# Head sums of squares of four feature tiles on 32 columns each of TensorE, and a product that orders the rows

## What is computed

```python
q = silu(short_conv(x @ Wq + bq, q_conv)).reshape(B, S, h, d)
q = q / (norm(q, axis=-1) + 1e-06)
k = silu(short_conv(x @ Wk + bk, k_conv)).reshape(B, S, h, d)
k = k / (norm(k, axis=-1) + 1e-06)
v = silu(short_conv(x @ Wv + bv, v_conv)).reshape(B, S, h, d)
alpha = sigmoid(x @ Wa + ba)
beta = sigmoid(x @ Wb + bb)
out_gate = silu(x @ Wg + bg)
```

## Time and profile before

| | us |
|---|---|
| median of 3 runs (lowest to highest) | 3533.43 (3529.58 to 3539.18) |
| the profiled execution's own time | 3535.1 |
| its span | 3533.3 |
| TensorE busy in the span | 3299.1 (93%) |
| VectorE busy | 2739.6 (78%) |
| ScalarE busy | 1582.4 (45%) |
| GpSimd busy | 1845.0 (52%) |

### The profile page before, as it was taken

How to read it: one execution, slowest core, us unless ns; L and a number is a source line. 1 busy time by engine, 2 the same in 40 slices (tenths; PEclk the granted TensorE clock), 3 DMA queues, 4 the chain that set the end, 5 groups by cost and what they waited for, 6 DMA issues and landing times. The chain is left out here.

```text
span 3533.3 us, 191423 instructions
## 1 busy us (share of the span) xinstructions
PE 3299.1 (93%) x83236; PEld 2757.8 (78%) x83236; DVE 2739.6 (78%) x4491; ACT 1582.4 (45%) x2344; POOL 1845.0 (52%) x1707
## 2 busy tenths in 40 slices
PE   7999998799999999995999999999996997999999
PEld 5888886576766767674999999999995775888887
DVE  6767665787888878784899999999997866676765
ACT  4555553577777777773112121111213433545454
POOL 1232322465555665654787887888785431323232
PEclk8999999899999999997999999999997998999999
DMA  3122222232322323225677777777774772212121
GB/s 119 71 95 83 88 90 91 78 100 78 102 79 84 101 74 99 86 76 133 182 200 202 198 200 199 197 197 200 197 200 136 238 226 107 107 71 107 71 107 60
DMA packets 486526, 452.84 MB, mean 128 GB/s; under 512 B 55489, under 2 KB 448833, under 8 KB 467265
## 3 DMA queue, kind: packets, MB, share of 16 engines
q1 hardware_dynamic: 484160, 449.56, 42.1%
q10 hardware_dynamic: 2304, 2.49, 0.3%
HBM read 331.33 MB, written 120.60 MB: 128 GB/s over the span
## 5 line engine op out<-in xcount | busy, mean ns | idle before, releaser
L350 POOL TENSOR_TENSOR ffn_out<-ffn_gate,ffn_xres 128x512 f32<-128x512 f32 x128 | 223.5, 1777 | 779.8 <-DVE ffn_gate L254 779.4
L784 DVE SCALAR_TENSOR_TENSOR ain_conv<-ain_padded,ain_taps,ain_conv 128x512 f32<-128x512 f32 x384 | 416.8, 1085 | 13.8 <-DVE ain_tail L781 0.3
L1464 ACT ACTIVATE rec_u<-rec_ps_end 128x256 f32<-128x256 f32 x128 | 49.2, 384 | 645.7 <-PE rec_ps_end L1516 645.7
L885 POOL TENSOR_TENSOR ain_conv<-ain_conv,ain_term 128x512 f32<-128x512 f32 x192 | 272.4, 1419 | 16.0
L1232 POOL TENSOR_TENSOR rec_d_norm<-rec_dmat,rec_early 128x512 f32<-128x512 f32 x128 | 162.9, 1273 | 181.6 <-DVE rec_dmat L1314 181.6
L940 ACT ACTIVATE ain_buf<-ain_conv 128x512 f32<-128x512 f32 x192 | 121.0, 630 | 233.5 <-POOL ain_conv L885 147.6
L46 PE MATMUL ffn_ring<-ffn_mixkh,ffn_wkh 128*128 128x512 f32 x512 | 218.7, 427 | 6.5 <-DVE ffn_mixkl L196 6.5
L46 PE MATMUL ffn_ring<-ffn_mixrh,ffn_wrh 128*128 128x512 f32 x512 | 216.0, 422 | 9.2 <-DVE ffn_mixrl L306 9.2
L46 PE MATMUL ffn_ring<-ffn_mixkh,ffn_wkl 128*128 128x512 f32 x512 | 203.8, 398 | 0.0
L46 PE MATMUL ffn_ring<-ffn_mixrh,ffn_wrl 128*128 128x512 f32 x512 | 202.6, 396 | 0.0
L46 PE MATMUL ffn_ring<-ffn_mixkl,ffn_wkh 128*128 128x512 f32 x512 | 201.7, 394 | 0.0
(11 more groups left out here) (249 smaller groups left out, 10351.9 us busy)
## 6 DMA issues: line engine op xcount, KB each, us to landing
rec_early<-coeffs SPq DMA_DIRECT2D x512, 128.0 KB, 3.0
streams<-ain_buf SPq DMA_DIRECT2D x48, 1024.0 KB, 5.1
rec_qkv<-streams SPq DMA_DIRECT2D x126, 384.0 KB, 3.3
rec_qk_pe<-streams SPq DMA_DIRECT2D x127, 256.0 KB, 3.3
rec_late<-coeffs SPq DMA_DIRECT2D x504, 64.0 KB, 2.2
ffn_xres<-in_x SPq DMA_DIRECT2D x16, 1024.0 KB
ain_x<-x SPq DMA_DIRECT2D x16, 1024.0 KB, 4.9
gate<-ain_gate SPq DMA_DIRECT2D x16, 1024.0 KB, 6.7
```

The costliest lines, as they stand in the source:

```text
L350: added = nc.gpsimd.tensor_tensor(out[:, m, :], gate[:, m, :], xres[:, m, :], ALU.add)
L784: nc.vector.scalar_tensor_tensor(out=out[:], in0=pad[:, n:n + TOK], scalar=taps[:, u // KT, u % KT, n:n + 1], in1=out[:], op0=ALU.mult, op ...
L885: nc.gpsimd.tensor_tensor(out[:], out[:], term[:], ALU.add).then_inc(pool_conv, 1)
L1464: nc.scalar.activation(u[:], ps_end[:, :, 1, :], ACT.Copy).then_inc(u_ready, 1)
```

## The change

The head sums of a kind (q, then k) are now made together, after group u = 8 and after group u = 12. The matmul of feature tile m is 32 columns wide and writes rows 32m to 32m + 31 of `ps_rows`: sums of q on its first four rows, of k on its next four. The four of k accumulate onto those of q, in other rows. `sq` has five tiles in place of four, so that k's first square doesn't overwrite one of q; from k's second on a square waits for q's four sums. ScalarE's root now takes all 128 partitions, into a new tile `root`. After group u = 13 TensorE multiplies `root` by a matrix of zeros and ones, `in_rows`, which brings the 32 wanted rows to partitions 32 to 63 of `ps_rows` (`order_rows`), and VectorE's norms wait for that (`rows_ordered`) and read `ps_rows`. `gamma_norm` now lies in the place of `alpha`. The new constants are made with fewer memsets and four small copies out of `ident`.

```diff
@@ -557,13 +557,13 @@
         taps = sb("taps", [P, 3, KT, TAPS])
         mean_w = sb("mean_w", [P, P])
         start_mask = sb("start_mask", [P, NT, 3 * KT, TAPS - 1])
-        head_sum = sb("head_sum", [P, 2 * KT, P])
+        head_sum, in_rows = sb("head_sum", [P, 2, HD]), sb("in_rows", [P, P])
         not_first = sb("not_first", [P, TOK])
         x = sb("x", [P, KT, TOK])
         xc = sb("xc", [P, KT, TOK])
         xh = [sb(f"xh{s}", [P, KT, TOK], F32R) for s in range(2)]
         xl = [sb(f"xl{s}", [P, KT, TOK], F32R) for s in range(2)]
-        sq = sb("sq", [P, 4, TOK])
+        sq = sb("sq", [P, 5, TOK])
         half, half2 = sb("half", [P, 2, TOK]), sb("half2", [P, 2, TOK])
         sum1, sum2 = sb("sum1", [P, TOK]), sb("sum2", [P, TOK])
         ident, ones = sb("ident", [P, P]), sb("ones", [P, P])
@@ -710,10 +713,15 @@
                 nc.vector.tensor_tensor(W[n][1][:], stage[n], W[n][0][:].bitcast(F32), ALU.subtract).then_inc(w_split[n], 1)
 
             def select_heads():
-                for n in range(2 * KT):
+
+
+                for j in range(2):
                     for h in range(HG):
-                        col = (2 + n // KT) * H + h * KT + n % KT
-                        last = nc.vector.memset(head_sum[h * HD:(h + 1) * HD, n, col:col + 1], 1.0)
+                        nc.vector.memset(head_sum[h * HD:(h + 1) * HD, j, j * HG + h:j * HG + h + 1], 1.0)
+                cols = in_rows[:, 2 * H:4 * H].rearrange("p (j h g) -> p j h g", j=2, h=HG)
+                for m in range(KT):
+                    rows = slice(m * HD, (m + 1) * HD)
+                    last = nc.vector.tensor_copy(cols[rows, :, :, m], ident[rows, m * HD:m * HD + 2 * HG].rearrange("p (j h) -> p j h", j=2))
                 last.then_inc(heads_selected, 1)
 
             def place_ab():
@@ -798,8 +806,8 @@
                 nc.vector.tensor_copy(gamma_end[HROWS, :], gamma[HROWS, CH - 1:TOK:CH]).then_inc(ends_ready, 1)
 
             def norms(t):
-                dve.wait_ge(rooted, t + 1)
-                nc.vector.tensor_scalar_add(inv_norm[HROWS, :], inv_norm[HROWS, :], 1e-6).then_inc(padded_norm, 1)
+                dve.wait_ge(rows_ordered, t + 1)
+                nc.vector.tensor_scalar_add(inv_norm[HROWS, :], ps_rows[HROWS, :], 1e-6).then_inc(padded_norm, 1)
                 dve.wait_ge(padded_norm, t + 1)
                 nc.vector.reciprocal(inv_norm[HROWS, :], inv_norm[HROWS, :]).then_inc(norm_ready, 1)
                 dve.wait_ge(norm_ready, t + 1)
@@ -940,13 +948,13 @@
                 nc.scalar.activation(view, conv[u % 3][:].rearrange("p (c i) -> p c i", i=CH), ACT.Silu).then_inc(silued, 1)
                 if j < 2:
                     act.wait_ge(silued, 12 * t + u + 1)
-                    if u >= 4:
-                        act.wait_ge(heads_summed, 8 * t + u - 3)
-                    elif more:
+                    if u > 4:
+                        act.wait_ge(heads_summed, 8 * t + 4)
+                    elif u < 4 and more:
                         act.wait_ge(halved2, t + 2)
                     else:
                         act.wait_ge(heads_summed, 8 * t)
-                    nc.scalar.activation(sq[:, u % 4, :].rearrange("p (c i) -> p c i", i=CH), view,
+                    nc.scalar.activation(sq[:, u % 5, :].rearrange("p (c i) -> p c i", i=CH), view,
                                          ACT.Square).then_inc(q_squared, 1)
 
             def slot(t, s, more):
@@ -969,7 +977,8 @@
                     if more and u == 10:
                         high(t + 1, 1 - s)
                 act.wait_ge(heads_summed, 8 * t + 8)
-                nc.scalar.activation(inv_norm[HROWS, :], ps_rows[HROWS, :], ACT.Sqrt).then_inc(rooted, 1)
+                act.wait_ge(rows_ordered, t)
+                nc.scalar.activation(root[:], ps_rows[:], ACT.Sqrt).then_inc(rooted, 1)
                 silu(t, 10, more)
                 act.wait_ge(gate_stored, 16 * t)
                 act.wait_ge(w_split["g"], 1)
@@ -1016,12 +1025,18 @@
                 nc.tensor.matmul(ps_rstd[:], ones[:], rstd_diag[:].rearrange("p j n -> p (j n)"), start=True,
                                  stop=True).then_inc(spread_done, 1)
 
-            def head_sums(t, n):
-                pe.wait_ge(q_squared, 8 * t + n + 1)
-                if n == 0:
-                    pe.wait_ge(rooted, t)
-                nc.tensor.matmul(ps_rows[:], head_sum[:, n, :], sq[:, n % 4, :], start=(n == 0),
-                                 stop=(n == 7)).then_inc(heads_summed, 1)
+            def head_sums(t, j):
+
+                if j == 0:
+                    pe.wait_ge(padded_norm, t)
+                for m in range(KT):
+                    pe.wait_ge(q_squared, 8 * t + KT * j + m + 1)
+                    nc.tensor.matmul(ps_rows[m * HD:(m + 1) * HD, :], head_sum[:, j, :], sq[:, (KT * j + m) % 5, :],
+                                     start=(j == 0), stop=(j == 1), skip_group_check=True).then_inc(heads_summed, 1)
+
+            def order_rows(t):
+                pe.wait_ge(rooted, t + 1)
+                nc.tensor.matmul(ps_rows[:], in_rows[:], root[:], start=True, stop=True).then_inc(rows_ordered, 1)
 
             def slot(t, s, more):
                 pe.wait_ge(x_low, t + 1)
@@ -1041,8 +1056,10 @@
                     product(nc, ring[u % 4][:], *W["qkvg"[j]], m, xh[s], xl[s]).then_inc(group_done, 1)
                     if u == 5:
                         pe.wait_ge(heads_selected, 1)
-                    if 5 <= u < 13:
-                        head_sums(t, u - 5)
+                    if u in (8, 12):
+                        head_sums(t, u // 4 - 2)
+                    if u == 13:
+                        order_rows(t)
                     if more and u == 7:
                         var(t + 1)
                     if more and u == 11:
```

More of the change, by code:

```diff
@@ L578, in attn_in_phase @@
         alpha, beta, inv_norm = sb("alpha", [P, TOK]), sb("beta", [P, TOK]), sb("inv_norm", [P, TOK])
-        decay, gamma, gamma_norm = sb("decay", [P, TOK]), sb("gamma", [P, TOK]), sb("gamma_norm", [P, TOK])
+        decay, gamma, root = sb("decay", [P, TOK]), sb("gamma", [P, TOK]), sb("root", [P, TOK])
+        gamma_norm = alpha
         gamma_end = sb("gamma_end", [P, CPT])
@@ L605, in attn_in_phase @@
         q_squared, heads_summed, rooted = sem("q_squared"), sem("heads_summed"), sem("rooted")
+        rows_ordered = sem("rows_ordered")
         decay_ready, first_ready, scanned, padded_norm, norm_ready = (
@@ L695, in _ @@
             nc.vector.memset(head_sum[:], 0.0)
+            nc.vector.memset(in_rows[:], 0.0)
             nc.vector.memset(wab_pad, 0.0)
@@ L835, in _ @@
             weight_high("k")
+            dve.wait_ge(ident_step, 2)
             select_heads()
-            dve.wait_ge(ident_step, 2)
             deviations(0)
@@ L905, in square @@
                 act.wait_ge(centred, t + 1)
-                nc.scalar.activation(sq[:], xc[:], ACT.Square).then_inc(squared, 1)
+                nc.scalar.activation(sq[:, 0:KT, :], xc[:], ACT.Square).then_inc(squared, 1)
             def deviation(t):
```

## The result

| | us |
|---|---|
| changed kernel, median of 4 runs | 3637.96 (3633.78 to 3641.40) |
| kernel before, median of 4 runs beside it | 3536.30 (3529.58 to 3544.31) |
| ratio, 95% interval | 1.0293 (1.0280 to 1.0306) |
| the profiled execution's span | 3636.3 |

The change makes the kernel 2.9% slower, 101.7 us. The forecast was +68 (3601, range 3556 to 3632): the direction held, the size didn't, and the time lies above the range.

A forecast was written before the change was run, and what follows sets the result against it. Bound by the chain of ScalarE's shifts and silus and GpSimd's units, not TensorE. Fourteen intervals of 2.0 + 2.2 us (59), the last 7 and the end 2 gave +68 us: 3601 us, range 3556 to 3632.

The forecast's parts named there:

- What bounds the kernel: Slot of 61.33 us: a chain of ScalarE's shifts and silus and GpSimd's units 2, 5, 8 sets the pace, not TensorE.
- Head sums: TensorE's narrow sums: 1.2 us for four instead of 0.96 us each; the saving beside the chain, worth nothing by itself.
- The wait for the root: TensorE after group 13: idle 5.9 us (3.3), GpSimd's unit 2 3.8 us later, part given back, net +2.0 us a slot.
- The clock: TensorE's clock falls after the idle time, before the groups unit 2 needs: +2.2 us a slot, bounds 0 and +3.0.
- Normalising earlier: VectorE's lost wait for the spread of 1/std, 32.8 us in 14 waits: counted as nothing, VectorE waiting for ScalarE instead.
- The sum: Root to root: fourteen intervals of 4.2 us make 59, the last 7, the end 2; together +68 us.
- The rival of +99: Slots: no relief on GpSimd (+3.3) and 3.0 us from the clock, 3632 us; chance 0.05.
- The faster rival: TensorE's own work is the bound: 4.3 us less over 15 slots, 65 us, 3468 us; chance 0.06.
- The memsets: Before the first slot: fewer memsets save VectorE up to 3.9 us, covered by GpSimd's sums; otherwise under 3 us once.

## Why the prediction was wrong in its size

*What bounds the kernel.* Right. TensorE's 94% were no bound: 1 to 2 us less of its work a slot gained nothing, once with slots of 61.7 us and once with 59.1.

*Head sums.* The 1.2 us taken for four was 1.1 measured, where they didn't wait for a square. The packing section of the Trainium skill's page "TensorE: Matmul & The Clock Gate" has 2.38 times for three tiles of 32 columns; the 1.6 us for four worked out from it was an estimate, and the runs show less, 1.1. What the forecast had wrong here is the saving: 7.7 - 2.4 - 0.96 = 4.3 us by its working, 1.8 measured, since the wide sum costs 0.86 us between groups and not 0.96, and since the narrow ones seldom stand ready all four. It decides nothing.

*The wait for the root.* The idle time was forecast at 5.9 us and measured at 6.4. Group 14 was forecast to start 5.04 us late, and against the root it starts 5.16 late. The step that failed is the next one: "groups 14 and 15, `ps_ab` and the next slot's groups" are not all that is queued behind the wait. The mean product stands among them, between group 0 and group 1, and VectorE's centring waits for it. My sum had its 0.85 us, as the one float32 product, but not its reader. I had both facts in the description of the kernel and followed only the queue's groups, to shift(2). There the delay arrived as 3.8 us, and I let 1.8 of it be given back, 1.3 by GpSimd's units and 0.5 by silu(2). At the centring it arrives whole, at the head of the slot, so that ScalarE, VectorE and GpSimd shift together and meet each other as before: unit 2 took 9.3 us in the changed kernel, not 8.6, and nothing is given back.

*The clock.* Right as a mechanism, 1.5 us a slot in place of 2.2 (the mean product's 6.5 us less the 5.04 of queueing, and 68.3 less 66.8 with TensorE kept at work). Its size doesn't follow the length of the wait: 2 slow matmuls behind 6.4 us in the changed kernel, 5 to 7 behind 5.5 us with the mean ahead, 6 to 14 behind 4.0 us with the wait alone. What sets it stays open.

*Normalising earlier.* I had counted nothing for VectorE's lost wait for the spread. It cost: unit 9 of VectorE, from 1104.46 to 1109.90, moved into GpSimd's unit 8, which runs in the changed kernel from 1100.18 to 1109.35, 9.17 us,

```profile
1100.18 0.64 POOL L883 COPY ain_padded<-ain_tail 128x3 f32<-128x3 f32 x1 [4.26 <-ACT ain_conv L937]
...
1107.75 1.60 POOL L893 TENSOR_TENSOR ain_conv<-ain_conv,ain_term 128x512 f32<-128x512 f32 x1
```

and before from 1121.93 to 1130.57, 8.64 us, with VectorE's unit 9 only from 1128.64 on. That is +0.5 us a slot. It fits the version with the ordering product behind group 15, whose unit 8 takes 9.17 us too and whose slots are 61.7 and not 61.3.

*The sum, put right.* 5.04 us of queueing and 1.5 of clock, less 0.1 that the mean was early, plus 0.5 on unit 8: 6.9 us a slot; measured 68.3 - 61.3 = 7.0. Fourteen of them make 98, the last interval 59.2 - 52.4 = 6.8 (7.2 forecast), the start gives 1.9 back: 103, which is the difference of the spans.

*The rival of +99* had nearly this time for a wrong reason: no relief on GpSimd and a clock of 3.0. The faster rival fell with the ordering product behind group 15: there TensorE waits for the root no more and has less work, and the time is that of before.

*The memsets.* I took their saving to be covered by GpSimd's sums. There was none to cover, since the four copies cost more than the memsets saved; the 1.9 us at the start have another source, as told with the result.

## What to carry to other kernels

When a wait is put into the queue of an engine, list every instruction behind it up to the next wait and name the reader of each, the small ones above all; the one that counts is the one whose reader opens the next round, not the one that is most of the work. Here one mean product of 0.85 us behind 48 matmuls carried the whole delay to all engines. And an engine at 94% that still waits for its inputs isn't the bound: up to 1.8 us a slot of its work taken away gained nothing, two sigmoids moved on an engine busy for 45% of the span gained 1.2%.

## What the runs showed of the hardware

Four float32 matmuls on 128 rows and 32 columns each, in different columns, take about the time of one: 8 records within 1.07 us, the next group 1.1 us after room was made, where one of 128 columns takes 0.96 to its successor. I had put four at 1.2 to 3.8.

Idle time on TensorE has a price behind it. With the wait of 4.0 us alone, 6 to 14 matmuls behind it ran at the lower clock, about 40 us in the whole kernel; with 12 needless matmuls in the gap, none did, and with 24 in its gap of 6.4 us the changed kernel became about 20 us faster. The Trainium skill's page "TensorE: Matmul & The Clock Gate", in its section on the clock's oscillation, says that waits between bursts of matmuls send the clock down each time, and these runs agree. Shorter waits did it too: with the ordering product behind group 15 no wait is longer than 2.1 us, and yet starts 0.43 us apart stand behind one of 2.09 us, with a granted clock of 0.97 over seven slots.

VectorE's unit 7 of three instructions on 128x512 took 2.33 us beside GpSimd's small copies and 4.64 us beside its wide instructions. Moving a step earlier on one of these two engines can cost the other more than it saves.
